# Attention heads written out with the causal mask added on VectorE, and two of four additions moved behind the weighing in the second experts

## The chip, the core and the metric

The kernel runs on one core of a Trainium2 chip. The metric is the device time of one execution in microseconds (us). Engines are called as the profile calls them: PE (TensorE, matrix products; PEld its weight loads), DVE (VectorE), ACT (ScalarE), POOL (GpSimd), SP (SyncE, which issues most transfers).

## The reference

A decoder of two layers with a layer norm behind each of six blocks, on x of 4 sequences x 256 tokens x 256 features. Cut to what matters:

```
x = layernorm(x + L0_attn(x))        # 16 heads of 128, rotary q and k, causal softmax
x = layernorm(x + L0_xattn(x, ctx))  # a decayed scan
x = layernorm(x + L0_ffn(x))         # 32 experts, 4 per token
x = layernorm(x + L1_attn(x))        # 16 heads, 4 key groups, causal softmax
x = layernorm(x + L1_xattn(x, ctx))
x = layernorm(x + L1_ffn(x))         # 8 fused experts, dense, below

# first attention, per head and sequence
p = softmax(where(causal, q @ k.T / sqrt(128), -1e30)); out = p @ v

# second experts, for each expert f
xe   = x + w_f @ muW_f.T
gate = silu(fused(xe, gW, gqa, gqb)); up = fused(xe, uW, uqa, uqb)
y   += scalar_f * fused(gate * up, dW, dqa, dqb)    # fused: a product plus a weighted low-rank one
```

## The kernel before

Every block of the program gives each engine its own list of instructions; the lists run in order and are tied together by semaphores alone. The order of the work is written by hand. Operands that need more than one pass are cut into a high and a low part, and `product` (lines 76 to 78) makes three products of them.

**First attention** (`layer0_attention`). The work goes head by head, and in a head by sequence, b = 0 to 3. A step b of PE is: the scores of sequence b (`Attend.scores`, lines 242 to 245); projections of the next head (`project`, six chunks: q0 and k0 beside b = 0, v0 and q1 beside b = 1, k1 and v1 beside b = 2, none beside b = 3; lines 76 to 78 and 411); the transposes of the probabilities of two steps before (`turn`, line 253); the product with v of three steps before (`mix`, lines 262 and 263). DVE takes the maxima of the scores (`maxima`, lines 270 and 271), rotates a projected chunk (`rotate_in`, lines 463 and 467), and divides the probabilities of the step before by their sum (`divide`, lines 285 to 288). ACT makes the exponentials (`exps`, lines 278 and 280), moves the transposed probabilities, the mixed values and v out of PSUM (lines 294, 301 and 540) and cuts the high part of the weights (line 546). POOL finishes the rotation (lines 510 and 514) and cuts the low part of the weights (line 519). The two chunk buffers in PSUM alternate: k1 goes where v0 was, so PE's projection of k1 waits for ACT's line 540.

In `Attend`, the mask is put into PSUM by a bf16 product of the identity with the mask on both diagonal blocks (line 242), and the scores are accumulated on top. `MaskedAttend`, which the second attention uses, has no such product: DVE adds the mask to the scores and takes the negated maximum in one instruction (line 322), which writes the probabilities' tile in SBUF; ACT then works in place there (lines 328 and 330).

The heads are emitted by `heads`: heads 0, 1, 14 and 15 are written out, heads 2 to 13 are a hardware loop of six turns with two heads in each, on every engine.

**Second experts** (`layer1_experts`). A unit n is one expert and one half of the tokens, 16 units in all; expert e is units 2e and 2e + 1. PE's order in unit n: `gate_up_lora(n)` (line 2612), `down_out(n - 1)`, `factors(n + 1)`, `down_input(n)`, `gate_up(n + 1, 0)`, `low_inputs(n + 2)` (lines 2582 and 2584), the rest of `gate_up(n + 1)`. `low_inputs(n + 2)` writes the PSUM tile that `down_input(n)` filled, so it waits until DVE has read it (`act1[KR:P]`, line 2773, called the weighing of the down factors here). ACT, at the end of an even unit, cuts the high parts of the next expert's weights (lines 2455 to 2471) behind `keep_xe` (line 2667) and ahead of the next unit's silu (line 2682). POOL cuts the low parts from there. DVE's order in unit n is in the diff below; `add` (line 2734, `add_last` line 2742 for the last unit) adds a quarter of the output of unit n - 1 to `k.y`, and `keep_xe` (line 2713) is what ACT's line 2667 waits for.

Of the kernel before, what the change touches and what calls it, by code (L numbers as in the profile page):

```python
# [8 lines left out]
P = 128  # L9
B, S, D = 4, 256, 256  # L10
# [5 lines left out]
H, HD = 16, 128  # L16
# [194 lines left out]
class Attend:  # L211
# [84 lines left out]
    def mixed_out(self, b, head):  # L296
        return self.k.ctxT[:, bass.ds(head, 1), b * S:(b + 1) * S].rearrange("p a s -> p (a s)")

# [35 lines left out]
def layer0_attention(nc, k, I):  # L334

    with ExitStack() as stack:
        m = Memory(nc, stack)
        ROT = 4
        w = m.sb("a0_w", [P, 2, 3, DC, HD])
# [7 lines left out]
        proj_ps = m.ps("a0_proj_ps", [P, 2, 512])  # L347
        at = Attend(m, k, "a0", k.y)
        squared = m.sem("a0_squared")
# [17 lines left out]

        def heads(eng, emit):

            emit(0, 0, 0, True, False, True)  # L370
            emit(1, 0, 1, False, False, True)
            with eng.Fori(1, H // 2 - 1) as pair:
                emit(2 * pair, pair, 0, False, False, True)
                emit(2 * pair + 1, pair, 1, False, False, True)
            emit(H - 2, H // 2 - 1, 0, False, False, False)
            emit(H - 1, H // 2 - 1, 1, False, True, False)

        with nc.Block() as block:
            @block.sync
            def _(sp):  # L380
                def load(h, par):
                    at_least(sp, v_proj, 2 * (h - 2) + 2)
                    for n, name in enumerate(("L0_attn_Wq", "L0_attn_Wk", "L0_attn_Wv")):
                        sp.dma_start(w[:, par, n], I[name][:, bass.ds(h * HD, HD)].rearrange("(c p) d -> p c d", p=P)
                                     ).then_inc(w_in[par], 16)
                load(0, 0)
                load(1, 1)
                load_rest(sp, k, I)
                with sp.Fori(1, H // 2) as pair:
                    load(2 * pair, 0)  # L390
                    load(2 * pair + 1, 1)

            @block.tensor
            def _(pe):
                def project(h, pair, par, c):
# [3 lines left out]
                    else:  # L399
                        pe.wait_ge(w_low, 2 * h + PIECE[what] + 1)  # L400
                    if isinstance(h, int) and h == 0:
                        pe.wait_ge(x_low, DC * (half + 1))
# [28 lines left out]
                def emit(h, pair, par, first, last, ahead):  # L431
                    for b in range(B):
# [12 lines left out]
                        elif not first:  # L445
                            mix(h - 1, 1 - par, B + b - at.MIX)
                heads(pe, emit)
                at.turn(pe, B * H - 2, B - 2)
# [6 lines left out]
            def _(dve):  # L455
# [33 lines left out]
                def emit(h, pair, par, first, last, ahead):  # L489
                    for b in range(B):  # L490
# [6 lines left out]
                        if b or not first:  # L497
                            at.divide(dve, n - 1, (b - 1) % B)
                heads(dve, emit)
                at.divide(dve, B * H - 1, B - 1)  # L500

            @block.gpsimd
            def _(pool):
# [23 lines left out]
                def emit(h, pair, par, first, last, ahead):  # L527
                    if ahead:
                        cut_low(h + 2, par)
                    if not last:  # L530
                        for c in NQK:
                            rotate(h + 1, c, 1 - par)
                heads(pool, emit)

            @block.scalar
            def _(act):
# [28 lines left out]
                def emit(h, pair, par, first, last, ahead):  # L565
                    for b in range(B):
# [8 lines left out]
                        if not last:  # L575
                            for c in BESIDE[b]:
                                if c in NV:

                                    at_least(act, at.mixed, 4 * h - 2 + 2 * CHUNKS[c][1])
                                    keep_v(h + 1, 1 - par, c)  # L580
                heads(act, emit)
                at.keep_turned(act, B * H - 2, B - 2)
# [1923 lines left out]
def layer1_experts(nc, k, I, O):  # L2506
# [3 lines left out]
    with ExitStack() as stack:  # L2510
# [37 lines left out]
        with nc.Block() as block:  # L2548
# [159 lines left out]
            def _(dve):  # L2708
# [17 lines left out]
                def weigh_rest(n):  # L2726
                    dve.wait_ge(aw_high, n + 1)
                    dve.tensor_tensor(aw_p.l[:, :], aw[:, :], aw_p.h[:, :], ALU.subtract).then_inc(aw_low, 1)
# [23 lines left out]
                for n in range(N):  # L2752
# [11 lines left out]
                    if n:  # L2764
                        for q in range(4):
                            if n + 1 < N:
                                add(n - 1, q)
                            else:
                                add_last(n - 1, q)
# [5 lines left out]
                    if n + 1 < N:  # L2775
                        weigh_rest(n + 1)
                    dve.wait_ge(awd_high, n + 1)
                    dve.tensor_tensor(act1_p.l[KR:P, n % 2, :], act1[KR:P, :], act1_p.h[KR:P, n % 2, :],
# [291 lines left out]
```

## Time and profile before

| what | value |
|---|---|
| time, median of 3 runs | 1152.67 us (1152.44 to 1154.89) |
| the profiled execution, its own time | 1150.72 us |
| its span, first to last instruction | 1148.8 us |
| busy PE / PEld / DVE / ACT / POOL | 1027.6 / 830.0 / 722.9 / 570.5 / 473.5 us |
| mean granted clock of TensorE | 0.951 of full speed |

The span is what the views of the trace cover; 1.9 us lie around it. Matrix products are pipelined: the profile gives each from its start to its modelled end, so neighbours overlap, and what one costs PE is the distance from its start to the next one's start.

### The profile page before, as it was taken

What the parts mean: (1) busy time and instruction counts of PE and PEld (TensorE: products, weight loads), DVE (VectorE), ACT (ScalarE), POOL (GpSimd) and SP (SyncE); (2) the same over time, 40 slices, a digit from 0 to 9 for tenths busy, and PEclk for the clock granted to TensorE, in tenths of its full rate; (3) what the DMA queues carried; (4) which work ended last, traced back from release to release, by engine and by line L of the source; (5) the groups of instructions that cost most, each with busy time, mean ns of one, the idle gap of its engine ahead of it and who ended that gap; (6) DMA issues with size and microseconds to landing.
All of it is one profiled execution on the core that took longest, in us unless ns stands there. A gap on an engine that the chain in (4) does not pass through costs nothing. (4 is left out here: it accounts for less than half of the span.)

```text
span 1148.8 us, 19245 instructions
## 1 busy us (share of the span) xinstructions
PE 1027.6 (89%) x6044; PEld 830.0 (72%) x6044; DVE 722.9 (63%) x2000; ACT 570.5 (50%) x1568; POOL 473.5 (41%) x507
## 2 busy tenths in 40 slices
PE   4999999999994599939899999988987889999995
PEld 3888888887883399917778888856444568787785
DVE  5878777776365356636665663115687648788775
ACT  2355445545222155426676773026775545655553
POOL 5776777673257544366211110010035313444322
PEclk9999999999997699969999999988998989999998
DMA  9600000000001499832401101001003011112101
GB/s 314 265 28 28 27 14 27 27 14 1 1 28 57 130 322 333 284 110 83 152 24 60 29 19 38 1 21 49 2 2 111 1 55 55 56 56 66 45 1 38
DMA packets 83481, 85.41 MB, mean 74 GB/s; under 512 B 8545, under 2 KB 75943, under 8 KB 83280
## 3 DMA queue, kind: packets, MB, share of 16 engines
q1 hardware_dynamic: 76944, 67.00, 18.3%
q10 hardware_dynamic: 3392, 10.16, 2.3%
q0 software_dynamic: 3072, 7.34, 2.1%
q8 instruction: 38, 0.62, 0.2%
q14 instruction: 35, 0.29, 0.1%
HBM read 63.36 MB, written 22.02 MB: 74 GB/s over the span
## 5 line engine op out<-in xcount | busy, mean ns | idle before, releaser
L514 POOL TENSOR_TENSOR a_qk<-h,a_by_sin 128x512 f32<-128x512 f32 x64 | 89.1, 1392 | 5.0
L294 ACT ACTIVATE a_probsT<-a_turn_ps 128x384 f32<-128x384 f32 x128 | 61.7, 482 | 43.4 <-PE a_turn_ps L253 43.4
L322 DVE CUSTOM_DVE_ANT_0 h<-a_score_ps,mask_bf 128x128 f32<-128x128 f32 (+1 forms) x128 | 40.8, 356 | 60.6 <-PE a_score_ps L315 60.0
L76 PE MATMUL a_proj_ps<-a_x_l,a_w_h 128*128 128x512 f32 x128 | 57.5, 449 | 16.9 <-POOL a_w_l L519 16.5
L1235 POOL TENSOR_TENSOR a_w_l<-a_w,a_w_h 128x256 fp32r<-128x256 f32 x30 | 21.9, 730 | 111.6 <-ACT a_w_h L1428 111.5
L278 ACT ACTIVATE y_moe<-a_score_ps,a_nmax 128x128 f32<-128x128 f32 x64 | 23.5, 368 | 87.5 <-DVE a_nmax L271 87.5
L411 PEld LDWEIGHTS a_proj_ps<-a_w,xT 128*128 128x128 f32 x512 | 62.6, 193 | 2.7 <-issue 0.5
L411 PE MATMUL a_proj_ps<-a_w,xT 128*128 128x128 f32 x512 | 62.8, 276 | 0.1
L974 POOL TENSOR_TENSOR e_w_l<-e_w,e_w_h 128x512 fp32r<-128x512 f32 x32 | 40.9, 1278 | 52.8 <-ACT e_w_h L1042 52.8
L699 PE MATMUL t_y_ps<-wo,attnT 128*128 128x256 f32 x256 | 57.2, 380 | 0.0
L2483 POOL TENSOR_TENSOR m_up_l<-m_up_w,m_up_h 128x1024 fp32r<-128x1024 f32 x8 | 19.4, 2426 | 90.0 <-ACT m_up_h L2455 90.0
L1475 PE MATMUL p_y_ps<-wo,attnT 128*128 128x256 f32 x256 | 55.5, 379 | 0.8 <-PEq L1207 0.8
L1475 PEld LDWEIGHTS p_y_ps<-wo,attnT 128*128 128x128 f32 x256 | 48.6, 190 | 7.5 <-issue 0.9
L287 DVE TENSOR_SCALAR y_moe<-y_moe,a_rtotal 128x128 f32<-128x128 f32 x64 | 52.3, 818 | 2.3
L699 PEld LDWEIGHTS t_y_ps<-wo,attnT 128*128 128x128 f32 x256 | 47.9, 190 | 6.1
L78 PE MATMUL a_proj_ps<-a_x_h,a_w_l 128*128 128x512 f32 x128 | 51.9, 405 | 0.0
L77 PE MATMUL a_proj_ps<-a_x_h,a_w_h 128*128 128x512 f32 x128 | 51.7, 404 | 0.0
L463 DVE TENSOR_TENSOR h<-a_proj_ps,cos_q 128x512 f32<-128x512 f32 x32 | 22.1, 692 | 44.7 <-PE a_proj_ps L78 44.7
L328 ACT ACTIVATE h<-h,a_nmax 128x128 f32<-128x128 f32 x64 | 25.7, 402 | 46.9 <-DVE a_nmax L322 44.2
L467 DVE STREAM_SHUFFLE hT<-a_proj_ps 128x512 f32<-128x512 f32 x64 | 47.1, 736 | 0.0
L510 POOL TENSOR_TENSOR a_by_sin<-hT,sin_q 128x512 f32<-128x512 f32 x32 | 40.9, 1279 | 14.1 <-DVE hT L467 14.1
L510 POOL TENSOR_TENSOR a_by_sin<-hT,sin_k 128x512 f32<-128x512 f32 x32 | 41.3, 1291 | 9.6 <-DVE hT L467 9.6
(436 smaller groups left out, 3383.2 us busy)
## 6 DMA issues: line engine op xcount, KB each, us to landing
slots<-zeros ACTq DMA_DIRECT2D x4, 2048.0 KB, 16.1
e_rows<-slots SPq DMA_DIRECT2D x32, 256.0 KB, 4.7
e_w<-in_L_ffn_w_dram SPq DMA_DIRECT2D x32, 256.0 KB, 4.8
out_slots<-e_out SPq DMA_DIRECT2D x32, 256.0 KB, 4.3
e_w<-in_L_ffn_w_dram SPq DMA_DIRECT2D x32, 128.0 KB, 4.3
a_w<-in_L_attn_w_q_dram SPq DMA_DIRECT2D x32, 128.0 KB
m_up_w<-in_up_dram SPq DMA_DIRECT2D x8, 512.0 KB, 4.0
a_w<-in_L_attn_Wq_dram SPq DMA_DIRECT2D x16, 128.0 KB, 2.2
```

The source lines that it names most:

```text
L76: pe.matmul(out, left[0], right[1], start=start, stop=False)
L77: pe.matmul(out, left[0], right[0], start=False, stop=False)
L78: return pe.matmul(out, left[1], right[0], start=False, stop=stop)
L287: dve.tensor_scalar(self.probs[:, b, 0:P], self.probs[:, b, 0:P], self.rtotal[:, b, 0:1], None, ALU.mult)
L294: act.activation(self.probsT[:, b % 2, :], self.turn_ps[:, b % 2, 0:CAUSAL], ACT.Copy).then_inc(self.turned_kept, 1)
L411: last = pe.matmul(proj_ps[:, c % 2, t * HD:(t + 1) * HD], k.xT[:, kc, half * HALF + t * P:half * HALF + (t + 1) * P], w[:, par, 2, kc, :] ...
L467: dve.stream_shuffle(swapped[:, r, :], proj_ps[:, c % 2, :], [i ^ 1 for i in range(32)]).then_inc(rot_in, 1)
L510: pool.tensor_tensor(by_sin[:, r2, :].rearrange("p (b s) -> p b s", b=2), swapped[:, r, :].rearrange("p (b s) -> p b s", b=2), sin[:, None ...
L514: pool.tensor_tensor(qk[:, par, 0 if what == "q" else 1, half * HALF:(half + 1) * HALF], by_cos[:, r, :], by_sin[:, r2, :], ALU.add).then_ ...
L699: last = pe.matmul(y_ps[:, t % 2, 0:D], k.ctxT[:, h, t * P:(t + 1) * P], k.wo[:, h, :], start=h == 0, stop=h == H - 1)
L974: pool.tensor_tensor(w13_p.l[:, r], w13[:, r], w13_p.h[:, r], ALU.subtract).then_inc(w_low, 1)
L1475: last = pe.matmul(y_ps[:, t % 2, 0:D], k.ctxT[:, h, t * P:(t + 1) * P], k.wo[:, h, :], start=h == 0, stop=h == H - 1)
```

## The change

In the first attention the class `Attend` is replaced by `MaskedAttend`; the loop over heads is written out on every engine, so that addresses and awaited counts are constants; nothing else in the order of the work there changes. In the second experts, DVE makes two of the four additions of the unit before where all four stood, and the other two behind `weigh_rest`.

```diff
     def mixed_out(self, b, head):
-        return self.k.ctxT[:, bass.ds(head, 1), b * S:(b + 1) * S].rearrange("p a s -> p (a s)")
+        return self.k.ctxT[:, head, b * S:(b + 1) * S]
...
-        at = Attend(m, k, "a0", k.y)
+        at = MaskedAttend(m, k, "a0", k.y)
...
-        def heads(eng, emit):
-
-            emit(0, 0, 0, True, False, True)
-            emit(1, 0, 1, False, False, True)
-            with eng.Fori(1, H // 2 - 1) as pair:
-                emit(2 * pair, pair, 0, False, False, True)
-                emit(2 * pair + 1, pair, 1, False, False, True)
-            emit(H - 2, H // 2 - 1, 0, False, False, False)
-            emit(H - 1, H // 2 - 1, 1, False, True, False)
+        def heads(emit):
+
+            for h in range(H):
+                emit(h, h // 2, h % 2, h == 0, h == H - 1, h + 2 < H)
...
-                with sp.Fori(1, H // 2) as pair:
-                    load(2 * pair, 0)
-                    load(2 * pair + 1, 1)
+                for h in range(2, H):
+                    load(h, h % 2)
...
                     if n:
-                        for q in range(4):
+                        for q in range(2):
                             if n + 1 < N:
                                 add(n - 1, q)
                             else:
                                 add_last(n - 1, q)
                     if n + 1 < N:
                         weigh(n + 1)
                     dve.wait_ge(dqa_done, n + 1)
                     dve.tensor_tensor(act1[KR:P, :], xe_ps[KR:P, 0, :], wrep[KR:P, n % 2, :], ALU.mult
                                       ).then_inc(awd_done, 1)
                     if n + 1 < N:
                         weigh_rest(n + 1)
+                    if n:
+                        for q in range(2, 4):
+                            if n + 1 < N:
+                                add(n - 1, q)
+                            else:
+                                add_last(n - 1, q)
                     dve.wait_ge(awd_high, n + 1)
```

## Rows read from the trace of the kernel before

**Rows 1.** Windows (A:B length, busy us of PE, PEld, DVE, ACT, POOL; clock): two heads.

```profile
85.51:101.87 16.36, 16.34 (x106) 14.31 (x105) 12.47 (x32) 8.27 (x28) 11.90 (x10) 1.00 0.09 26
101.87:118.23 16.36, 16.35 (x105) 14.31 (x104) 12.38 (x32) 8.27 (x28) 11.96 (x11) 1.00 0.08 24
```

**Rows 2.** Timeline (start us, us long), PE around the mask's product.

```profile
124.39 0.27 PE L242 MATMUL a_score_ps<-mask_bf,ident_bf 128*128 128x256 bf16 x1
124.49 0.39 PE L244 MATMUL a_score_ps<-a_qk 128*128 128x128 f32 x2
```

**Rows 3.** Timeline of the same head, from step 1's transposes to k1's projection.

```profile
118.23 0.49 PE L253 MATMUL a_turn_ps<-ident,y_moe 128*128 128x128 f32 x3
...
119.32 0.39 PE L244 MATMUL a_score_ps<-a_qk 128*128 128x128 f32 x2
...
119.41 0.60 ACT L540 ACTIVATE a_v<-a_proj_ps 128x512 f32<-128x512 f32 x1
...
120.16 0.47 PE L76 MATMUL a_proj_ps<-a_x_l,a_w_h 128*128 128x512 f32 x1
```

**Rows 4.** Timeline, DVE from there to the transposes of step 3.

```profile
119.95 1.36 DVE L287 TENSOR_SCALAR y_moe<-y_moe,a_rtotal 128x128 f32<-128x128 f32 x1
...
121.50 0.28 DVE L270 TENSOR_REDUCE a_nmax<-a_score_ps 128x1 f32<-128x128 f32 x1
...
122.03 0.68 DVE L463 TENSOR_TENSOR h<-a_proj_ps,cos_k 128x512 f32<-128x512 f32 x1
...
124.72 0.34 DVE L288 TENSOR_SCALAR y_moe<-y_moe,a_rtotal 128x256 f32<-128x256 f32 x1
...
125.15 0.51 PE L253 MATMUL a_turn_ps<-ident,y_moe 128*128 128x128 f32 x3
```

**Rows 5.** Second attention, timeline and one line's spread (min/median/max ns).

```profile
614.29 0.29 DVE L322 CUSTOM_DVE_ANT_0 h<-a_score_ps,mask_bf 128x128 f32<-128x128 f32 x1 [1.39 <-PE a_score_ps L315]
...
614.85 0.16 DVE L285 RECIPROCAL a_rtotal<-a_total 128x2 f32<-128x2 f32 x1
```

```profile
L322 DVE CUSTOM_DVE_ANT_0 h<-a_score_ps,mask_bf x128: 277/354/425, 518.8 to 694.9; 128x128 f32<-128x128 f32 x64, 128x256 f32<-128x256 f32 x64
```

**Rows 6.** The page, part 5: groups, busy us, mean ns, idle before.

```profile
L278 ACT ACTIVATE y_moe<-a_score_ps,a_nmax 128x128 f32<-128x128 f32 x64 | 23.5, 368 | 87.5 <-DVE a_nmax L271 87.5
...
L328 ACT ACTIVATE h<-h,a_nmax 128x128 f32<-128x128 f32 x64 | 25.7, 402 | 46.9 <-DVE a_nmax L322 44.2
```

**Rows 7.** Who waited for whom, PE, second experts: total us, times, longest.

```profile
PE m_xe_ps L2582 <- DVE m_act L2773: 2.5, 7, 0.4
```

**Rows 8.** Timeline of an odd unit of the second experts, DVE and PE.

```profile
1007.45 1.05 DVE L2762 TENSOR_TENSOR m_act_l<-m_act,m_act_h 64x512 fp32r<-64x512 f32 x1
...
1008.42 1.64 DVE L2734 SCALAR_TENSOR_TENSOR y_moe<-m_down_ps,scalar,y_moe 128x256 f32<-128x256 f32 x4
...
1008.88 0.39 PE L76 MATMUL m_xe_ps<-m_act_l,m_dqa_h 128*128 128x512 f32 x1
...
1010.69 0.69 DVE L2773 TENSOR_TENSOR m_act<-m_xe_ps,m_wrep 64x512 f32<-64x512 f32 x1
...
1010.70 0.39 PE L78 MATMUL m_gu_ps<-m_xe_h,m_up_l 128*128 128x512 f32 x1
...
1011.44 0.73 PE L2582 MATMUL m_xe_ps<-softT,m_mu 128*128 128x512 f32 x2 [0.36 <-DVE m_act L2773]
```

**Rows 9.** Timeline of the even unit before it, into the odd one.

```profile
999.77 1.29 DVE L2713 TENSOR_TENSOR m_xe<-m_xe_ps,xT 128x512 f32<-128x512 f32 x2
...
1001.63 1.04 ACT L2455 ACTIVATE m_up_h<-m_up_w 128x1024 fp32r<-128x1024 f32 x1
...
1003.92 0.57 ACT L2682 ACTIVATE m_silu<-m_gu_ps 128x512 f32<-128x512 f32 x1
```

**Rows 10.** Timeline of the last unit.

```profile
1133.34 0.69 DVE L2773 TENSOR_TENSOR m_act<-m_xe_ps,m_wrep 64x512 f32<-64x512 f32 x1
...
1134.73 0.69 DVE L2778 TENSOR_TENSOR m_act_l<-m_act,m_act_h 64x512 fp32r<-64x512 f32 x1 [0.69 <-ACT m_act_h L2693]
```

More of the change, by code:

```diff
@@ L383, in load @@
                     for n, name in enumerate(("L0_attn_Wq", "L0_attn_Wk", "L0_attn_Wv")):
-                        sp.dma_start(w[:, par, n], I[name][:, bass.ds(h * HD, HD)].rearrange("(c p) d -> p c d", p=P)
+                        sp.dma_start(w[:, par, n], I[name][:, h * HD:(h + 1) * HD].rearrange("(c p) d -> p c d", p=P)
                                      ).then_inc(w_in[par], 16)
@@ L400, in project @@
                         pe.wait_ge(w_low, 2 * h + PIECE[what] + 1)
-                    if isinstance(h, int) and h == 0:
+                    if h == 0:
                         pe.wait_ge(x_low, DC * (half + 1))
@@ L446, in emit @@
                             mix(h - 1, 1 - par, B + b - at.MIX)
-                heads(pe, emit)
+                heads(emit)
                 at.turn(pe, B * H - 2, B - 2)
@@ L498, in emit @@
                             at.divide(dve, n - 1, (b - 1) % B)
-                heads(dve, emit)
+                heads(emit)
                 at.divide(dve, B * H - 1, B - 1)
@@ L532, in emit @@
                             rotate(h + 1, c, 1 - par)
-                heads(pool, emit)
+                heads(emit)
             @block.scalar
@@ L580, in emit @@
                                     keep_v(h + 1, 1 - par, c)
-                heads(act, emit)
+                heads(emit)
                 at.keep_turned(act, B * H - 2, B - 2)
```

## The prediction

> **What bounds the kernel now.** I read the window sums first, to see which engine fills a stretch. In a middle head of the first attention PE is busy for 16.34 us of 16.36 at the full clock, DVE for 12.5, ACT for 8.3, POOL for 11.9 [rows 1]. So PE's list sets the pace there, and an instruction taken from it is worth its step, unless PE then waits for somebody. Second, the timeline, to see where PE's starts stand further apart than its products need. One place in a head shows it, and one more is only just not a wait; both are costed below. Third, the list of waits for the second experts. PE waits there seven times for DVE's weighing (L2773), 2.5 us in all [rows 7]; that is once in an odd unit, units 1 to 13. All else in those units runs product behind product. Last, the chain that leads into such a wait, through DVE, back to ACT and the unit before [rows 8, 9].
>
> **The mask's product.** It starts at 124.39 and the next product at 124.49 [rows 2]: its span says 0.27 us, but it takes 0.10 of PE's time. 64 of them (16 heads, 4 sequences) are 6.4 us. That is the most this edit can give. Whether it gives it is a matter of what PE meets next, and the four steps of a head differ.
>
> Step 2: PE starts the transposes of step 1 at 118.23, and the score products of step 2 at 119.32. These take 0.66 (as from 124.49 to 125.15 in step 3) [rows 2, 4], so PE is free at 119.98, yet k1's projection starts at 120.16 [rows 3]: it waits for the buffer that ACT's L540 empties until 120.01. ACT's three copies follow PE's transposes of 118.23, no later score. Without the mask's product PE comes 0.10 sooner and waits 0.28 in place of 0.18. This mask gives nothing.
>
> Step 3: DVE has no idle time from L287 at 119.95 to the end of L288 at 125.06, and PE's transposes of sequence 1, which need L288, start at 125.15 [rows 4]. L287 alone takes 1.36 us there, as POOL works beside it. This chain of DVE starts from q1's projection, which ends at 118.23, so it does not move when masks go. PE alone would arrive at 125.15 - 0.20 (two masks) + 0.10 (the longer wait of step 2) = 125.05. DVE will release it at 125.15 or a little later. This mask gives nothing either.
>
> Steps 0 and 1: I find no such release close by (the turned probabilities and the rotated chunks are ready more than a microsecond ahead), so each gives its 0.10.
>
> **DVE and ACT in the other class.** Two reductions become two instructions that add, write and reduce. Before, from L270 at 121.50 to the next work of DVE at 122.03: 0.53 us [rows 4]. In the second attention, from L322 at 614.29 to the next at 614.85: 0.56 [rows 5]. So +0.03 per sequence, and in step 2 it lies on the DVE chain above. ACT's exponential of 128 columns takes 402 ns from SBUF against 368 from PSUM [rows 6], and I take the same 0.03 for the second one: +0.07 per sequence, 4 x 0.07 = 0.3 per head, on an engine that is idle for 8 of 16.4 us. It is hidden by ACT's wait for PE's transposes. Were that cover gone in step 2, PE would lose 0.07 more per head, 1.1 us in all. The new wait of `maxima` for the transposes of four sequences before has been met long ago in PE's order; the wait of the scores for `maxed` in place of `exped` comes earlier than the old one.
>
> The Trainium skill (VectorE: DVE Perf Modes, section Rules for kernel authors) calls the plain reduction the slowest operation of DVE and advises to restructure it. By that the pair would get shorter, step 3's wait would shrink, and up to 15 x 0.10 = 1.5 us more would come out. The rows above say 0.03 longer, and I go by them.
>
> Per head: two masks at 0.10, less 0.03 = 0.17. For the 15 heads that have a next head beside them: 2.5 us. The last head has no projections; its scores, maxima, exponentials and copies run in a ring in which 0.10 less on PE stands against 0.03 + 0.07 more on DVE and ACT: nothing. **First attention: -2.5 us**, with bounds of 0 and -6.4.
>
> **The loop written out.** Inside the loop's body a head takes 16.36 us (the window from 85.51), and across a back edge also 16.36 (from 101.87) [rows 1]. So branches, register addresses and counts cost PE nothing that can be given back; SP's loads are a head ahead. I take 0. The other side, longer instruction lists to fetch: the second experts are written out already, and PE waited there for engines alone in the middle units [rows 7], so 0 again. The code for ten more heads is the only new thing.
>
> The Trainium skill (Runtime: NRT & Kernel Launch, section Instruction fetch mechanics) says that a taken branch to outside a small window of instructions stalls the engine on a fetch, and that this speaks for unrolling. By that rule each of the six back edges would have cost something. The two equal windows don't show it. It is a rival below.
>
> **The additions.** Four take 1.64 us, so two take 0.8 [rows 8]. In an odd unit the weighing starts at 1010.69, and PE's L2582 at 1011.44, 0.74 behind its last product at 1010.70. From 1008.88 to 1010.70 are eight steps, so 0.23 is the usual one: 0.51 lost. With two additions fewer the weighing is 0.8 nearer, or as soon as `down_input` is done, and this wait goes: 7 x 0.51 = 3.6 us.
>
> But the other two additions now stand ahead of `keep_xe` (L2713). In an even unit DVE is without idle time from the weighing to L2713, and the weighing itself waits for PE and can't come sooner. So L2713 moves from 999.77 by 0.8. Behind it ACT runs without a gap: L2667, the cuts from L2455 at 1001.63, and then the odd unit's silu at 1003.92 [rows 9], although PE had the gate ready before. Everything of the odd unit moves by 0.8: silu, act, its low part L2762, which ends at 1008.50 and whose reader on PE starts at 1008.88 [rows 8]. Cover is 0.38, less some 0.05 for the signal. So PE will wait there for 0.8 - 0.33 = 0.45. POOL's cuts follow ACT's and move too, so who is held by whom stays as it is. This happens in units 3 to 13, six times; unit 0 has no additions, so unit 1 keeps its full gain. Sum: unit 1 -0.51, six times (0.45 - 0.51) = -0.4. In the last unit the weighing comes at 1133.34 behind four additions, and ACT and L2778 at 1134.73 follow [rows 10]; between 0 and 0.8 of it comes free, and I take the middle, 0.4, as PE's product ahead of the weighing must end too. The two additions moved there are hidden by ACT's 0.69. Later additions hold `down_out` only a unit later, microseconds off. **Second experts: -1.3 us**, with bounds of -4.4 (3.6 + 0.8: no wait in place of the old one) and +2.4 on top of the forecast (six units that lose 0.4 more, as much again as the new wait).
>
> **Sum.** -2.5 - 1.3 = -3.8 against the profiled execution's own 1150.72 (span 1148.8 and 1.9 around it): 1146.9. The median shown is 1.95 above it, so 1152.67 - 3.8 = 1148.9 us.
>
> **Rivals.**
> 1. More comes out: the wait of step 3 or the one in the odd units does not take the saving. For it: both covers are worked out to a tenth only, and POOL's place beside L287 may change (L287 varies widely where POOL works). Against: both chains are without a gap in the trace. All masks at 6.4 with the experts as forecast: 1152.67 - 7.7 = 1145.0. Experts in full with the attention as forecast: 1152.67 - 2.5 - 4.4 = 1145.8. Both: 1141.9. Chance 0.17.
> 2. Nothing is left: the additions lose 0.1 more in each odd unit than I count, and steps 0 and 1 meet waits I don't see. DVE is busy for 12.5 of 16.4 and POOL for 11.9, so a ring of the two is possible. About 1152.67 - 0.5 = 1152.2. Chance 0.21.
> 3. Slower: the new instruction of DVE is held by POOL as L287 is. At 121.50 POOL is at work. L287 takes 1.36 there, where L288 with twice the columns takes 0.34 [rows 4], so about 1.0 more would lie on step 3's chain in each of 15 heads: 15 x (1.0 + 0.03 - 0.20) = +12.5, with the experts 1163.9. It decides from a delay of some 0.25 us per head on. Against it: of 128 such instructions in the second attention none took over 0.425 us [rows 5], though POOL is less busy there, and L463, which also reads PSUM and SBUF and writes SBUF, takes its 0.68 beside POOL [rows 4]. Chance 0.06.
> 4. The written-out lists cost fetches, on an engine with a short cover: a few tenths per head, 1152 to 1157. Chance 0.05.
> 5. The back edges did cost something on an engine other than PE, by the rule above: each of six gives back less than the equal windows can hide, 0.05 or so, and the time is within 0.3 of the forecast. Chance 0.03 on top of the forecast's own 0.48.
>
> **How the numbers follow.** The forecast, 1148.9, has 0.48; its own range is 1147 to 1150.8. The range reaches down to cover the single forms of rival 1, not both together, and up past rival 2 to the start of rival 4: 1144.5 to 1153.5. Outside lie rival 3, half of rival 4 and a part of rival 1. What can be told from no change is about 0.2%, 2.3 us. Faster by more: rival 1, rival 5 and most of the forecast, 0.63. Within: rival 2, a little of the forecast, 0.25. Slower: rival 3 and most of rival 4, with a mixture in which the additions lose more, 0.12.
>
> **What would show it.** No L242 in the first attention; a head's period of about 16.19 in place of 16.36; L76 of k1 still at 1.93 behind the transposes of step 1, with a longer idle time; the transposes of step 3 still at 6.92 to 6.98 behind those of step 1, released by L288. L322 in the first attention at 0.29 and 0.42, never near 1.3. In the experts: L2582 no longer held in an odd unit; ACT's L2682 0.8 later against PE's last product of the gate; a new idle time of 0.3 to 0.4 ahead of the second product group of `down_input`, released by L2762; 24.9 us for two units, as before, but for the first pair. The prediction is wrong if a period falls by 0.4, if the two units fall to 24.4, or if DVE waits for POOL in a new place.

## The result, and the profile after

The changed kernel takes 1148.28 us (median of 11 runs, from 1143.31 us up) against 1152.67 us for the kernel before (11 runs): a ratio of 0.9956, 95% interval 0.9937 to 0.9975, which is 2.9 to 7.3 us. The forecast was 1148.9. One of the eleven runs, of 3543.89 us, was disturbed and is left out of the ratio (the median without it is 1148.00 us), as is one run each of mask01 and mask2 below. The profiled execution has a span of 1145.9 us, 2.9 below that of before.

Line numbers behind the first attention's loop are lower by 6 now (L463 is L457, L540 is L534, L2582 is L2576, L2773 is L2767). Two heads in the windows view, with the columns of [rows 1]:

```profile
85.30:101.40 16.10, 15.98 (x102) 13.93 (x101) 12.69 (x40) 8.48 (x28) 11.97 (x11) 1.00 0.09 25
101.40:117.50 16.10, 15.98 (x102) 13.93 (x101) 12.69 (x40) 8.48 (x28) 11.95 (x11) 1.00 0.09 26
```

A head takes 16.10 us where it took 16.36; the forecast was 16.19. Four masks left PE's list, some 0.10 us each, yet only 0.26 us came out, and PE is idle for 0.12 a head where it was for 0.02. The timeline of the same stretch as [rows 3, 4], from the transposes of step 1 at 118.10 to those of step 3 and the product behind them:

```profile
117.87 0.39 PE L78 MATMUL a_proj_ps<-a_x_h,a_w_l 128*128 128x512 f32 x1
118.10 0.49 PE L253 MATMUL a_turn_ps<-ident,y_moe 128*128 128x128 f32 x3
118.30 0.69 DVE L457 TENSOR_TENSOR h<-a_proj_ps,cos_q 128x512 f32<-128x512 f32 x1 [1.86 <-PE a_proj_ps L78]
...
119.28 0.60 ACT L534 ACTIVATE a_v<-a_proj_ps 128x512 f32<-128x512 f32 x1
...
119.73 1.36 DVE L287 TENSOR_SCALAR y_moe<-y_moe,a_rtotal 128x128 f32<-128x128 f32 x1
...
120.03 0.47 PE L76 MATMUL a_proj_ps<-a_x_l,a_w_h 128*128 128x512 f32 x1
...
121.28 0.28 DVE L322 CUSTOM_DVE_ANT_0 y_moe<-a_score_ps,mask_bf 128x128 f32<-128x128 f32 x1
...
123.25 1.36 DVE L287 TENSOR_SCALAR y_moe<-y_moe,a_rtotal 128x128 f32<-128x128 f32 x1
123.25 1.27 POOL L504 TENSOR_TENSOR a_by_sin<-hT,sin_k 128x512 f32<-128x512 f32 x1 [0.76 <-DVE hT L461]
123.27 0.49 PE L253 MATMUL a_turn_ps<-ident,y_moe 128*128 128x128 f32 x3
...
124.53 0.34 DVE L288 TENSOR_SCALAR y_moe<-y_moe,a_rtotal 128x256 f32<-128x256 f32 x1
...
124.93 0.55 PE L253 MATMUL a_turn_ps<-ident,y_moe 128*128 128x128 f32 x3
...
125.31 0.38 PE L262 MATMUL a_mix_ps<-a_probsT,a_v 128*128 128x256 f32 x1
```

Of the kernel before, the rows that answer to them and that [rows 3, 4] don't have:

```profile
118.00 0.39 PE L78 MATMUL a_proj_ps<-a_x_h,a_w_l 128*128 128x512 f32 x1
...
118.52 0.69 DVE L463 TENSOR_TENSOR h<-a_proj_ps,cos_q 128x512 f32<-128x512 f32 x1 [2.19 <-PE a_proj_ps L78]
...
123.40 0.49 PE L253 MATMUL a_turn_ps<-ident,y_moe 128*128 128x128 f32 x3
...
125.50 0.60 PE L262 MATMUL a_mix_ps<-a_probsT,a_v 128*128 128x256 f32 x2
```

k1's projection still starts 1.93 us behind the transposes of step 1 (120.03 - 118.10), held by ACT's copy of v0, so the mask of step 2 gave nothing, as forecast. Step 3 is where the head beat the forecast. Its transposes come 6.83 us behind those of step 1; before it was 6.92 and the forecast was 6.92 to 6.98. All of the difference lies between the transposes of step 2 and those of step 3, where the mask of step 3 was: 1.75 us before (123.40 to 125.15), 1.66 here (123.27 to 124.93). The division came sooner as well. DVE's rotation of q1 (118.30) starts 0.43 us behind the start of PE's last product (117.87). Before it was 0.52 us (118.52 behind 118.00), in each of the 24 rotations of q inside the loop, and 0.43 in those of the heads outside it that waited for PE. From that start to the transposes of step 3 the chain of DVE takes 6.63 us in both kernels. PE is now held by this division for a few hundredths, and pays for it behind the transposes: their step to the next product is 0.38 us (125.31 - 124.93), before it was 0.35, and where PE has not waited it is 0.33. This longer first step behind a wait is called the restart below.

The new instruction is not held by POOL. The page has all 128 of them (the two widths together) at a mean of 351 ns (355 in the second attention):

```profile
L322 DVE CUSTOM_DVE_ANT_0 y_moe<-a_score_ps,mask_bf 128x128 f32<-128x128 f32 (+1 forms) x128 | 40.3, 351 | 13.2 <-PE a_score_ps L315 13.2
```

One head went worse in this execution. In head 1, both divisions of sequence 1 ran beside POOL, and PE waited 0.67 us for the second:

```profile
59.07 1.27 POOL L504 TENSOR_TENSOR a_by_sin<-hT,sin_k 128x512 f32<-128x512 f32 x1
...
59.12 1.37 DVE L288 TENSOR_SCALAR y_moe<-y_moe,a_rtotal 128x256 f32<-128x256 f32 x1
...
60.55 0.55 PE L253 MATMUL a_turn_ps<-ident,y_moe 128*128 128x128 f32 x3 [0.67 <-DVE y_moe L288]
```

From the transposes of one head to those of the next, against the kernel before: head 0 +0.08 us, head 1 +0.58, heads 2 to 12 together -3.03, head 13 -0.11, the last two heads +0.27. Sum -2.2: PE's last transposes of the first attention start at 281.93 us (before 284.12). The forecast had -2.5. The first two heads don't repeat, though: attn_only and even4 below have the same first attention, and in their profiled executions head 0 took 17.94 and 16.00 us, head 1 16.12 and 16.02 (here 15.75 and 16.93). In add_only, whose first attention is that of the kernel before, head 0 took 17.70 where it was 15.67. From head 2 on the sum is -2.9 us.

In the second experts PE's list of waits no longer names the weighing (L2767), which it did seven times [rows 7]. It names L2756 instead, the low part of `act`:

```profile
PE m_down_ps L76 <- DVE m_act_l L2778: 2.4, 1, 2.4
PE m_xe_ps L76 <- DVE m_act_l L2753: 1.4, 1, 1.4
PE m_xe_ps L76 <- DVE m_act_l L2756: 1.1, 6, 0.2
```

The timeline of the even unit and the odd one behind it shows the chain that leads there [compare rows 8, 9]:

```profile
995.95 0.88 DVE L2728 SCALAR_TENSOR_TENSOR y_moe<-m_down_ps,scalar,y_moe 128x256 f32<-128x256 f32 x2
996.86 0.69 DVE L2778 TENSOR_TENSOR m_act_l<-m_act,m_act_h 64x512 fp32r<-64x512 f32 x1
997.58 1.29 DVE L2707 TENSOR_TENSOR m_xe<-m_xe_ps,xT 128x512 f32<-128x512 f32 x2
...
1002.33 0.69 DVE L2749 TENSOR_TENSOR m_act<-m_silu,m_gu_ps 128x512 f32<-128x512 f32 x1 [2.06 <-ACT m_silu L2676]
...
1005.26 1.05 DVE L2756 TENSOR_TENSOR m_act_l<-m_act,m_act_h 64x512 fp32r<-64x512 f32 x1
```

```profile
1005.22 0.51 PE L76 MATMUL m_xe_ps<-m_act_l,m_dqa_h 128*128 128x512 f32 x1
1005.55 0.40 PE L77 MATMUL m_xe_ps<-m_act_h,m_dqa_h 128*128 128x512 f32 x1
1005.79 0.40 PE L78 MATMUL m_xe_ps<-m_act_h,m_dqa_l 128*128 128x512 f32 x1
1006.36 0.50 PE L76 MATMUL m_xe_ps<-m_act_l,m_dqa_h 128*128 128x512 f32 x1 [0.17 <-DVE m_act_l L2756]
1006.70 0.40 PE L77 MATMUL m_xe_ps<-m_act_h,m_dqa_h 128*128 128x512 f32 x1
```

The two additions behind the weighing take 0.91 us to the next instruction (995.95 to 996.86). On PE, the first product of `down_input` starts 0.34 us behind the one before it and the second group 0.57, where 0.23 is usual, and the step after each of these restarts is 0.33 or 0.34. The start of unit n's `act` on DVE repeats every 25.10 us for two units, before every 24.98. On PE, units 0 and 1 together gained 0.60 us, the six pairs behind them lost 0.12 each, the tail gained 0.43: -0.3 us in all, where the forecast had -1.3.

### The profile page after: what moved, and what is told of

Same layout as the page of the kernel before. It is cut to its first block and busy times, and to the rows that moved or that the text cites. A ratio compares the mean times of both kernels' runs of the same rounds, so it can differ in the third digit from the quotient of the medians.

```text
span 1145.9 us, 18712 instructions
## 1 busy us (share of the span) xinstructions
PE 1026.5 (90%) x5980; PEld 825.4 (72%) x5980; DVE 731.6 (64%) x2128; ACT 572.9 (50%) x1568; POOL 476.2 (42%) x507
## 5 line engine op out<-in xcount | busy, mean ns | idle before, releaser
L294 ACT ACTIVATE a_probsT<-a_turn_ps 128x384 f32<-128x384 f32 x128 | 61.2, 479 | 39.6 <-PE a_turn_ps L253 39.6
L322 DVE CUSTOM_DVE_ANT_0 h<-a_score_ps,mask_bf 128x128 f32<-128x128 f32 (+1 forms) x128 | 40.8, 355 | 59.1 <-PE a_score_ps L315 58.9
L328 ACT ACTIVATE y_moe<-y_moe,a_nmax 128x128 f32<-128x128 f32 x64 | 25.8, 402 | 86.2 <-DVE a_nmax L322 85.2
L287 DVE TENSOR_SCALAR y_moe<-y_moe,a_rtotal 128x128 f32<-128x128 f32 x64 | 55.1, 861 | 2.3
L322 DVE CUSTOM_DVE_ANT_0 y_moe<-a_score_ps,mask_bf 128x128 f32<-128x128 f32 (+1 forms) x128 | 40.3, 351 | 13.2 <-PE a_score_ps L315 13.2
L457 DVE TENSOR_TENSOR h<-a_proj_ps,cos_q 128x512 f32<-128x512 f32 x32 | 22.1, 691 | 37.2 <-PE a_proj_ps L78 37.2
L76 PEld LDWEIGHTS a_proj_ps<-a_x_l,a_w_h 128*128 128x128 f32 x128 | 25.1, 196 | 28.9 <-POOL a_w_l L513 17.5
```

The source lines that it names most:

```text
L76: pe.matmul(out, left[0], right[1], start=start, stop=False)
L287: dve.tensor_scalar(self.probs[:, b, 0:P], self.probs[:, b, 0:P], self.rtotal[:, b, 0:1], None, ALU.mult)
L294: act.activation(self.probsT[:, b % 2, :], self.turn_ps[:, b % 2, 0:CAUSAL], ACT.Copy).then_inc(self.turned_kept, 1)
L322: done = dve.tensor_tensor_reduce(self.probs[:, b, cells], self.score_ps[:, r, cells], self.k.mask_bf[:, cells], -1.0, 3e38, ALU.add, ALU. ...
L328: act.activation(self.probs[:, b, 0:P], self.probs[:, b, 0:P], ACT.Exp, bias=self.nmax[:, b, 0:1], scale=-1.0, accum_out=self.total[:, b, ...
```

## The experiments

Twelve kernels ran. Ratios are to the kernel before, measured beside it on the same chip; its medians there were 1153.92 us (first four kernels), 1153.85 (next four) and 1153.44 (last four). "Period" is a middle head of the first attention on the timeline, "pair" two middle units of the second experts. Periods and pairs are read from one profiled execution each.

### The two parts apart

**add_only.** The kernel before, and of the change only this:

```diff
-                        for q in range(4):
+                        for q in range(2):
...
+                    if n:
+                        for q in range(2, 4):
+                            if n + 1 < N:
+                                add(n - 1, q)
+                            else:
+                                add_last(n - 1, q)
```

> The kernel before with only the additions moved. Theory of the prediction: unit 1 gains 0.5, units 3 to 13 trade one wait for another, the tail gains 0.4: -1.3 us. Theory after reading the changed profile: the first pair gains 0.56, six pairs of units lose 0.12 each (25.10 us a pair in place of 24.98), the tail gains 0.43: -0.3 us, no difference that can be told. Rival: the wait is gone for good, 24.4 us a pair and -4 us.

Measured: 1153.58 us, ratio 0.9994 (0.9975 to 1.0013). A pair takes 25.13 us, no wait for the weighing is left, and six waits for the low part of `act` are there, as in the changed kernel. The moved additions give nothing that can be told from the spread.

**attn_only.** The changed kernel with all four additions ahead of the weighing.

> The changed kernel with the additions put back. Head period 16.11 us in the first attention, as in the changed kernel; experts at 24.98 us a pair. Theory: the whole gain is the attention's, so -2.2 to -4.1 us against before. Rival: the experts carry half of it, and this is -1.5 us.

Measured: 1148.59 us, ratio 0.9959 (0.9937 to 0.9981), period 16.10, pair 24.98 with the seven old waits. The ratio is that of the whole change (0.9956), so its gain is that of the first attention.

**loop_only.** The loop written out, the mask still PE's product.

> The kernel before with the heads written out but the mask still on PE. Theory of the prediction: nothing on PE, period 16.36 us. Theory after reading: DVE's instruction that waits for PE's projection starts 0.43 us behind the start of the last product in place of 0.52, as it does in the changed kernel and in head 14 of the kernel before, but PE is its own bound here, so the period stays at 16.33 to 16.36 and the time within 0.5 us. Rival (a taken branch costs a fetch): -2 us or more.

Measured: 1152.3 us, ratio 0.9987 (0.9968 to 1.0005), period 16.35. DVE's rotation starts 0.43 us behind PE's last product here too, and its division ends 0.09 us sooner, yet the transposes of step 3 stay at 6.92: with the mask's products in its list PE is not there earlier. Written out alone, the loop gives nothing.

**mask_dve.** DVE's mask, only DVE's list written out; PE, ACT, POOL and SP keep the loop.

> The kernel before with the mask added by DVE; only DVE's list of heads is written out, those of PE, ACT, POOL and SP keep their loop. Theory: DVE's waits for a count held in a register are what costs 0.09 us on the chain to the transposes of step 3, so the period is 16.11 us as in the changed kernel. Rival (the loops of the other engines matter): 16.2 us, as the prediction had it for the masks alone.

Measured: 1151.03 us, ratio 0.9978 (0.9959 to 0.9996). The windows view of one head:

```profile
104.00:120.08 16.08, 15.88 (x102) 13.93 (x101) 12.67 (x41) 8.56 (x28) 11.92 (x11) 1.00 0.08 24
```

16.08 us with the loop left on PE, ACT, POOL and SP, so of the written-out lists DVE's is enough. Its rotation starts 0.43 us behind PE's last product and its division ends 6.76 us behind the transposes of step 1, as in the changed kernel (6.77). But the 16.08 is put together in another way. ACT in the loop starts its copy 0.39 us behind PE's last transpose instead of 0.31, so that k1's projection comes at 2.00 us and the transposes of step 3 at 6.87 to 6.89. The division is done by then, PE does not wait for it, and the step behind these transposes is 0.33 in place of 0.38. The median is 2.4 us above that of attn_only, whose period is the same; the two intervals overlap, and nothing in the first attention explains it. The other half, DVE's mask with DVE still in the loop, was not tried, so that 0.09 us would be missing there is argued and not shown.

### Where a mask's product costs something

Both kernels are the changed one with the old product ahead of the scores in some steps of each head, so the mask is added twice there. The diff is mask01's; mask2 has `b in (2,)`:

```diff
+        again = b in (0, 1)
+        if again:
...
+            pe.matmul(diagonals, k.ident_bf[:, :], k.mask_bf[:, :].rearrange("p (a s) -> p a s", a=3)[:, ::2, :],
+                      start=True, stop=False, skip_group_check=True)
+        pe.matmul(self.score_ps[:, r, 0:P], q(0, P), key(0, P), start=not again, stop=True, skip_group_check=again)
...
```

**mask01.**

> The changed kernel with PE's mask product put back in steps 0 and 1 of each head, on top of DVE's mask, so that the mask is added twice there and the instruction sequence of DVE, ACT and POOL is the new one. My theory: the two products lie on PE's own path between the turn of step 3 and the turn of step 1, where PE's order decides, and each costs its own 0.10 to 0.11 us: the period of a head goes from 16.10 to 16.31 us, the attention is 3.2 us longer, the kernel at about 1151.5 us, where the chip of the run before gave 1148.6 for the changed attention. Rival (the gain of the attention comes from DVE's or ACT's new order, not from PE's products): the period stays at 16.10 and the time at about 1148.5.

**mask2.**

> The changed kernel with PE's mask product put back in step 2 of each head alone (the mask is added twice there). My theory: behind it PE comes to the projection of k1, which is released by ACT's copy of v0 (1.93 us behind the turn of step 1, before and after the change); PE waits 0.28 us there, so that the product is eaten by that wait: period 16.10 us, time as the changed kernel within its error. Rival (every PE instruction counts, the PE is the bound throughout): the period is 16.20 us and the time 1.6 us longer.

Windows, mask01 first and mask2 in the second fence:

```profile
107.45:123.76 16.31, 16.19 (x105) 14.12 (x104) 12.67 (x41) 8.48 (x28) 11.93 (x11) 1.00 0.09 26
```

```profile
107.96:124.06 16.10, 16.09 (x104) 14.02 (x103) 12.69 (x41) 8.48 (x28) 11.96 (x11) 1.00 0.09 26
```

mask01 has 16.31: 0.21 us for two products, all of it in the period. mask2 has 16.10: PE is busy for 0.11 more (16.09 against 15.98) and the period has not moved. The product fell into the wait. The total times don't fit my numbers. mask01 took 1154.95 us (ratio 1.0006, 0.9984 to 1.0028), where I expected 1151.5; mask2 took 1151.57 us (0.9973, 0.9954 to 0.9992). I had overlooked that the second attention uses the same class, so the products went in there as well. The first attention of mask01 ends 2.5 us later than in the changed kernel. What the products cost in the second is not shown: from its first to its last scores it takes 179.1 us in mask01 and 182.0 in mask2, and 175.8 to 179.6 in nine profiled kernels in which it is one and the same code.

### The additions, only where they help

**even4.** The changed kernel, with the halves in odd units only:

```diff
-                        for q in range(2):
+                        for q in range(2 if n % 2 else 4):
...
-                    if n:
+                    if n % 2:
                         for q in range(2, 4):
```

> The changed kernel, with the additions of the second experts in the old place (all four ahead of the weighing) in the even units, and halved as in the change only in the odd units. My theory: in the even units two additions behind the weighing push the next unit's act1 late, and PE's down_input waits for it (0.12 us on its first product and 0.35 us on its second group, and 0.11 us of restart on each); with all four ahead in the even units nothing is late there, and in the odd units the halves still keep the old wait for the weighing away. So both waits are gone: a pair of units takes about 24.4 us where it took 25.10 (and 24.98 before), six pairs give 4.4 us, the kernel at about 1144 us. Rival 1 (the waits come back at another place, the old one of even units ahead of low_inputs, as DVE's total work in a pair is what bounds): a pair stays at 24.9 to 25.1 us and the time at 1148. Rival 2 (half): the second group's wait stays since it stems from the odd unit's halves: 24.7 us a pair, 1146 us.

Measured: 1144.01 us, ratio 0.9909 (0.9887 to 0.9932), span 1141.4. PE's waits from 936 us on, then the timeline of the unit that answers to the one above:

```profile
PE m_down_ps L76 <- DVE m_act_l L2778: 2.4, 1, 2.4
PE m_xe_ps L76 <- DVE m_act_l L2753: 1.4, 1, 1.4
```

```profile
1000.80 0.69 DVE L2749 TENSOR_TENSOR m_act<-m_silu,m_gu_ps 128x512 f32<-128x512 f32 x1 [2.07 <-ACT m_silu L2676]
...
1003.72 1.05 DVE L2756 TENSOR_TENSOR m_act_l<-m_act,m_act_h 64x512 fp32r<-64x512 f32 x1
...
1006.18 0.69 DVE L2767 TENSOR_TENSOR m_act<-m_xe_ps,m_wrep 64x512 f32<-64x512 f32 x1
```

```profile
1004.94 0.39 PE L78 MATMUL m_xe_ps<-m_act_h,m_dqa_l 128*128 128x512 f32 x1
1005.16 0.39 PE L76 MATMUL m_xe_ps<-m_act_l,m_dqa_h 128*128 128x512 f32 x1
...
1007.20 0.62 PE L2576 MATMUL m_xe_ps<-softT,m_mu 128*128 128x512 f32 x2
```

Both waits are gone, the old and the new, and product follows product at 0.22 or 0.23 us. A pair takes 24.33 us (about 24.4 expected). So the old wait cost 24.98 - 24.33 = 0.65 us in a pair and the new ones 25.10 - 24.33 = 0.77; the change had traded one for the other. Against the changed kernel the ratio is about 0.9909 / 0.9956 = 0.9953 (the two were measured on different chips).

### What held PE in the first attention

**divide_v.** The changed kernel with two orders changed: DVE divides step n-1 right behind the maxima of step n, ahead of its rotation, and ACT copies v0 out (L534) in step 1 ahead of its copies of turn and mix.

```diff
                         at.maxima(dve, n, b)
+                        if b or not first:
+                            at.divide(dve, n - 1, (b - 1) % B)
                         if not last:
                             for c in BESIDE[b]:
                                 if c in NQK:
                                     rotate_in(h + 1, c)
-                        if b or not first:
-                            at.divide(dve, n - 1, (b - 1) % B)
...
+                        if b == 1 and not last:
+                            at_least(act, at.mixed, 4 * h - 2)
+                            keep_v(h + 1, 1 - par, 2)
```

> The changed kernel, with two orders of the first attention changed: DVE divides the probabilities of step n-1 right behind the maxima of step n, before it rotates; and ACT copies v0 out in step 1 before its two copies of turn and mix. My theory: these two chains (ACT's copy of v0, 1.93 us behind the turn of step 1, and DVE's division that ends 6.7 us behind it) are what kept the mask of step 2 and 3 from being worth anything; without them only PE's own order is left: the 0.28 us of waiting ahead of k1's projection and what is left of the wait for the division go, the period is 15.7 to 15.8 us, 0.3 to 0.4 less, so the kernel is 4.5 to 5.5 us faster than the changed one, about 1143.5 us. Rival (another chain is right behind, for one ACT's copy of the turned probabilities that the mix needs, now later by the 0.6 us of the copy of v0, or POOL's rotation): the period stays above 16.0 us and the time at 1148.

Measured: 1141.34 us, ratio 0.9884 (0.9852 to 0.9917), span 1139.7. Windows, and the timeline from the transposes of step 1 (114.84) on:

```profile
103.96:119.63 15.67, 15.67 (x102) 14.09 (x101) 12.16 (x40) 8.60 (x28) 11.66 (x11) 1.00 0.09 27
```

```profile
116.29 0.58 PE L76 MATMUL a_proj_ps<-a_x_l,a_w_h 128*128 128x512 f32 x1
...
121.28 0.49 PE L253 MATMUL a_turn_ps<-ident,y_moe 128*128 128x128 f32 x3
```

```profile
117.55 0.29 DVE L287 TENSOR_SCALAR y_moe<-y_moe,a_rtotal 128x128 f32<-128x128 f32 x1
117.76 0.34 DVE L288 TENSOR_SCALAR y_moe<-y_moe,a_rtotal 128x256 f32<-128x256 f32 x1
```

PE is busy for all of its 15.67 us. k1's projection comes at 1.45 us instead of 1.93, step 3's transposes at 6.44 instead of 6.83, and the division ends at 3.26, three microseconds ahead of need. Heads 1 and 13 also have 15.67 now. The attention ends at 274.12 us, 7.8 below the changed kernel.

**divide_first** and **v_first** make one half of that each.

> The changed kernel with only DVE's division ahead of its rotation. My theory: with 6.82 us from the turn of step 1 to that of step 3, PE's own order is the bound and the division ends just ahead of it; the 0.28 us of waiting for the copy of v0 stay: period 16.09 to 16.10 us in the middle heads, nothing gained there; what may go are the stalls of head 1 and head 13, 1.2 us together, since the held divisions then have slack: 1147.5 us. Rival (DVE's division is the bound of both places): period about 15.9 us, 1145 us or less.

> The changed kernel with only ACT's copy of v0 ahead of its copies of turn and mix in step 1. My theory: this one wait is the whole of the 0.43 us a head that divide_v gained; DVE's chain starts from the projection of k1 and so moves forward with it: period 15.67 to 15.72 us, about 1142.5 us. Rival (DVE's division becomes the bound once PE is 0.4 us earlier): period 15.85 to 16.0 us, 1146 us.

divide_first: 1145.98 us, ratio 0.9938 (0.9916 to 0.996). The period is 16.03 (16.09 expected): PE's transposes of step 3 come at 6.81 instead of 6.83, and the 0.05 us of a restart behind a wait (0.55 us for L253 at 124.93 above, 0.49 without) is saved as well. Head 1 has 16.03 too, head 13 also. v_first refuted my theory: 1147.93 us, ratio 0.9937 (0.9911 to 0.9962), and in the profiled execution periods of 16.08 to 16.11 in heads 3 to 12. Its timeline, PE and then DVE with POOL, from the transposes of step 1 at 118.73:

```profile
120.18 0.58 PE L76 MATMUL a_proj_ps<-a_x_l,a_w_h 128*128 128x512 f32 x1
...
125.57 0.33 PE L253 MATMUL a_turn_ps<-ident,y_moe 128*128 128x128 f32 x1 [0.24 <-DVE y_moe L288]
```

```profile
123.90 1.35 DVE L287 TENSOR_SCALAR y_moe<-y_moe,a_rtotal 128x128 f32<-128x128 f32 x1
125.17 0.34 DVE L288 TENSOR_SCALAR y_moe<-y_moe,a_rtotal 128x256 f32<-128x256 f32 x1
```

k1's projection does come at 1.45, but DVE's division, which starts together with POOL's product at 123.90 and takes 1.35 us instead of 0.29, now ends 6.78 us behind step 1's transposes and takes the place of the old wait. In head 1 it took 0.287 us, ended at 6.22, and that head had 15.67. So the two waits stand one behind the other: either edit alone gives 0.00 to 0.07 us of the period, both give 0.43.

**pe_mask_dv.** The kernel before, loop written out, mask still PE's product, with both orders of divide_v.

> The kernel before with the loop of the first attention written out, its mask still added by PE's product in all four steps, DVE's maxima and ACT's exponentials as before, but with the two orders of the run divide_v (division first, v0 copied out first). My theory: what a mask product costs depends only on whether PE waits behind it; with ACT's copy of v0 out of the way all four lie bare, 0.42 us a head, so the period is 15.67 + 0.42 = 16.09 us, where the same kernel without the two orders had 16.35: about 1148 us on a chip where before has 1153.5. Rival (something else than the products was gained by DVE's mask, such as the score buffers that come free at the maxima instead of the exponentials): the period is 16.2 us or more.

```profile
106.05:122.14 16.09, 16.09 (x106) 14.47 (x105) 11.96 (x32) 8.31 (x28) 11.67 (x11) 1.00 0.09 25
```

Measured: 1147.79 us, ratio 0.9953 (0.9932 to 0.9975), period 16.09 as expected. Against divide_v's 15.67 that is 0.42 us for four masks, 0.105 each: with nobody to wait for, every one of them counts.

The same in a table: one middle head, cut at the starts of PE's transposes. Each stretch holds the scores of one step, and so its mask where PE adds it.

| kernel | step 2 | step 3 | step 0 | step 1 | period |
|---|---|---|---|---|---|
| before | 5.17 | 1.75 | 4.52 | 4.92 | 16.36 |
| changed | 5.17 | 1.65 | 4.47 | 4.81 | 16.10 |
| mask_dve | 5.23 | 1.64 | 4.40 | 4.81 | 16.08 |
| divide_first | 5.17 | 1.64 | 4.41 | 4.81 | 16.03 |
| divide_v | 4.80 | 1.64 | 4.42 | 4.81 | 15.67 |
| pe_mask_dv | 4.91 | 1.75 | 4.52 | 4.91 | 16.09 |

The last two rows differ by a mask in each stretch, 0.10 or 0.11 us. Against the kernel before, the change has this in steps 3 and 1 in full, in step 0 less the 0.05 us of the restart behind the wait for the division, and in step 2 not at all: 0.10 + 0.11 + 0.05 = 0.26.

**best.** All three orders on the changed kernel.

> The changed kernel with all three orders of the runs before: division ahead of the rotation, v0 copied out first, and all four additions ahead of the weighing in even units. My theory: the two places have nothing to do with each other, so the gains add: 15.67 us a head and 24.33 us a pair of units, 1141.3 less 4.5 = about 1137 us, 1.4 to 1.6% below the kernel before. Rival (the 7 us of the first attention were partly luck of where the clock steps down, and do not add): 1140 us or more.

Measured: 1137.63 us, ratio 0.9847 (0.9816 to 0.9879), span 1135.5, period 15.67, pair 24.33. It beats both kernels, and the gains add.

## Why the prediction was right, step by step

- **A mask is worth 0.10 us where PE waits for nobody: right.** 0.105 each (mask01, and pe_mask_dv against divide_v).
- **Steps 0 and 1 give, step 2 gives nothing: right.** mask01 puts back 0.21 us, mask2 nothing. Of step 0's share 0.05 us went back into PE's restart behind the wait of step 3, which the sum did not have.
- **Step 3 gives nothing: wrong.** The stretch became 0.10 us shorter. "DVE will release it at 125.15 or a little later" had the right chain and a release that was too late. PE took 1.75 us there by its own list, mask included: loop_only, whose division ends 0.18 us ahead of the transposes, has the same 1.75. And DVE's chain began 0.09 us sooner once its list was written out. "So branches, register addresses and counts cost PE nothing that can be given back" held for PE (16.36 to 16.35 in loop_only), but I had read the windows for PE alone. Neither half is worth anything by itself: loop_only has DVE's 0.09 and gains nothing, and with DVE in its loop the release would come at some 6.91 us (an estimate: the division's end at 6.83 before, 0.02 for the new instructions, 0.06 from its end to PE's start in the changed kernel). That is 0.26 a head in place of 0.17. Of the 0.42 us taken from PE, 0.11 went into the wait of step 2 and 0.05 into the restart.
- **The new instructions, 0.03 us on DVE's chain: right, 0.02.** From L322 at 121.28 to L457 at 121.83 are 0.55 us, before 0.53 [rows 4].
- **Rule and trace on the back edge.** The Trainium skill (Runtime: NRT & Kernel Launch, section Instruction fetch mechanics) has a taken branch out of a small window stall on a fetch. A head without a back edge had the 0.09 us as well as one with it, so what was seen is not that stall; it went with the loop body as such. Whether the register address, the count in the wait or something else of the body costs it is open.
- **The 15 heads at one price: mis-sized.** The last two heads lost 0.27 us, in even4 and attn_only too, where the sum had a gain of 0.17 for one and nothing for the other. Why they lost it was not followed up. Head 1 lost 0.58 in this execution. By the prediction's own list of signs this counts against it: DVE was held beside POOL in a new place (L288 of sequence 1, 1.37 us; 0.34 in the kernel before). But attn_only has the same code, and there L288 took 0.34 at that place and the head 16.12 us, so the code alone does not decide it. What does is open; with the division first (divide_first) the head has 16.03.
- **The additions, -1.3 us: mis-sized, -0.3.** The mechanism was as described, with the new wait at the place named and in six pairs. "So PE will wait there for 0.8 - 0.33 = 0.45" was too small: the two additions take 0.91, not 0.8, so the second group of `down_input` came 0.91 - 0.33 = 0.58 us late (0.12 ahead of the first group, 0.11 in the restart behind that, 0.35 ahead of the second). The restart behind the second group adds 0.11, which the sum had at nothing, `low_inputs` 0.05 and the other steps 0.03: 0.77 in all. The old wait had a restart too (0.65 instead of 0.51). The sign of the trade was wrong, +0.12 a pair instead of -0.06; only the first two units (-0.60, forecast -0.51) and the tail (-0.43, forecast -0.4) gave something. Alone the part is 0.9994.
- **Rivals.** Of rival 1 the wait of step 3 did let the saving through (0.10, of which 0.05 went back), the one in the odd units did not. The written-out lists showed no wait for instructions (4), though the instruction queues carried 1.09 MB instead of 0.91. DVE's new instruction was not held (3). Rival 5 named what the 0.09 us were, a cost of the loop on an engine other than PE, though not of a back edge.
- **Where rule and trace met on the reduction.** By the Trainium skill (VectorE: DVE Perf Modes, section Rules for kernel authors) the plain reduction is what to get away from; the pair that replaced it takes 0.55 us against 0.53, so DVE gained nothing by it. The gain was PE's.

The two profiled executions differ by 3.0 us (1150.72 to 1147.72) where the sum had 3.8: -2.2 in the attention, -0.3 in the experts, and -0.5 elsewhere that no step claims. The medians differ by 4.4, and the 2.5 us of the two steps lie just outside the interval of 2.9 to 7.3. That the total was met to 0.6 us (1148.28 against 1148.9) was in part luck: the two steps gave 2.5 us where the sum had 3.8, and the rest came from places that no step names and from the spread of the executions.

## What to carry to other kernels

An instruction taken off the busy engine is worth its step only up to the next release; write down for each place who comes last and by how much, for DVE's chain as carefully as for PE's own. Two tight waits in a row hide each other: v_first and divide_first show near nothing in the period alone, together 0.43 us a head, more than the 0.26 that the change itself gave. Before moving work behind a wait, look at what stands behind it in every unit; here the same move helped in odd units and hurt in even ones, and a condition on n % 2 was worth about as much again as the whole change (0.9909 with it, 0.9956 without).

## What the runs showed of the hardware

- An instruction of DVE that waits for PE starts 0.52 us behind the start of PE's last product inside the hardware loop and 0.43 outside. For ACT's L294 it is 0.39 in mask_dve and 0.31 in the changed kernel, though in the kernel before, also a loop, it was 0.31; so it isn't the loop by itself. This stays open.
- L287, from SBUF to SBUF, takes 1.36 us where POOL's product starts at the same moment (both at 123.25 above), 0.7 us where it starts 0.7 us into POOL's product of 1.28 (ten middle heads of the changed kernel), and 0.29 us in divide_v, where 0.2 us of a product of POOL are left. It ends at or just behind the end of POOL's product each time. L322 and L457, which read PSUM and one operand in SBUF, were not seen held (0.28 and 0.68 us beside POOL's work). This agrees with the Trainium skill (SBUF — State Buffer, section SBUF: two separate sides), by which DVE and GpSimd take turns at one shared pair of ports for whole instructions.
- PE's restart behind a wait costs a product of 512 columns 0.10 us more in its next step (0.33 or 0.34 instead of 0.23), also where the view shows a wait of 0.17 us only, or none (1005.22, 0.11 us late). Behind three transposes it is 0.05 us (0.38 instead of 0.33).
